# Edge terms of a graph attention stage made one stage earlier, and added by the gathers that fetch keys and values

## The reference

```python
h = relu(layernorm(x))
logit = tanh(h @ W1.T) @ w2                      # "pool" round
x = x + segment_sum(softmax_by_dst(logit[src]) * h[src], dst)
h = relu(layernorm(x))
# "multi" round: 8 heads of 16
q, k, v = h @ Wq0 + bq0, h @ Wk0 + bk0, h @ Wv0 + bv0
e = edge_attr @ We0                              # 200,000 x 16 by 16 x 128
alpha = sum(q[dst] * (k[src] + e)) / 4           # per head
h = relu(segment_sum(softmax_by_dst(alpha) * (v[src] + e), dst) + h @ Ws0 + bs0)
# "single" round: the same with one head of 128, then the sum with x
```

## Time and profile before

| | us |
|---|---|
| median of 3 runs | 8751.74 (8746.28 to 8770.22) |
| profiled execution, its own time | 8750.25 |
| its span, first to last instruction | 8748.3 |
| PE busy | 6293.5 (72%) |
| DVE busy | 5246.4 (60%) |
| POOL busy | 4508.2 (52%) |
| ACT busy | 2808.0 (32%) |
| mean granted TensorE clock | 0.816 |

### The profile page before, as it was taken

The page is one execution under the profiler, slowest core; times in us unless marked ns, Lnnn a source line. Parts: engine busy times, 40 slices in busy tenths (PEclk is TensorE's granted clock), DMA queues, the critical chain, the costliest instruction groups (busy, mean ns, idle before and its releaser), DMA issues. The chain is left out here.

```text
span 8748.3 us, 177087 instructions
## 1 busy us (share of the span) xinstructions
PE 6293.5 (72%) x37309; PEld 4520.2 (52%) x37309; DVE 5246.4 (60%) x16838; ACT 2808.0 (32%) x6528; POOL 4508.2 (52%) x4707
## 2 busy tenths in 40 slices
PE   3455565566643678787787888865778888899998
PEld 2445555555531455555555555542455555555555
DVE  5344444455555888899998998863333444444452
ACT  2222233333310233333333333321333334444441
POOL 0566666666620566655554444411556666666550
PEclk6677777888876788888888888876888989999995
DMA  2333333333333444433333333334344444444442
GB/s 60 76 73 73 75 74 76 79 79 80 81 87 108 114 109 107 107 103 101 98 96 92 92 94 86 88 85 115 86 90 91 95 96 100 100 104 107 105 101 59
DMA packets 1195650, 796.51 MB, mean 91 GB/s; under 512 B 629426, under 2 KB 1086096, under 8 KB 1194616
## 3 DMA queue, kind: packets, MB, share of 16 engines
q0 software_dynamic: 175168, 411.90, 19.0%
q1 hardware_dynamic: 1019448, 373.53, 18.2%
HBM read 715.50 MB, written 69.42 MB: 90 GB/s over the span
## 5 line engine op out<-in xcount | busy, mean ns | idle before, releaser
L686 POOL DMA_INDIRECT ring_multi<-kv_rows,src_cols x1564 | 1549.9, 991 | 1722.0 <-DVE kv L794 492.0
L1085 POOL DMA_INDIRECT ring_single<-h_rows,src_cols x1564 | 1477.4, 945 | 1275.1 <-DMA ring_single<-h_rows,src_cols 470.7
L1085 POOL DMA_INDIRECT ring_pool<-pool_rows,src_cols x1564 | 1478.5, 945 | 1004.1 <-issue 421.3
L1198 PE MATMUL ps_s_pool<-ident,row_pool 128*128 128x128 f32 x1952 | 398.5, 341 | 875.8 <-issue 854.0
L1159 DVE CUSTOM_DVE_ANT_0 masked_pool<-mask_pool,ps_s_pool,start_pool 128x512 f32<-128x512 bf16 x488 | 364.6, 747 | 846.1 <-issue 787.4
L922 PE MATMUL ps_e_multi<-w_edge,attrT 64*128 64x512 f32 x976 | 591.3, 688 | 258.7 <-DVE kv L794 256.1
L1198 PEld LDWEIGHTS ps_s_pool<-ident,row_pool 128*128 128x128 f32 x1952 | 277.6, 173 | 962.4 <-issue 961.7
L1245 ACT ACTIVATE row_pool<-ring_pool 128x520 f32 x488 | 309.0, 633 | 1415.4 <-POOLq L1076 1415.4
L1213 PE MATMUL ps_p_pool<-row_pool,probT_pool 128*128 128x129 f32 x3904 | 714.5, 342 | 61.9 <-DVE probT_pool L1172 60.1
L905 PE MATMUL ps_p_multi<-message_multi,onehot 128*128 128x136 f32 x3904 | 729.7, 347 | 0.8 <-issue 0.8
L1213 PEld LDWEIGHTS ps_p_pool<-row_pool,probT_pool 128*128 128x128 f32 x3904 | 654.9, 253 | 104.0 <-issue 103.6
(11 more groups left out here) (219 smaller groups left out, 12509.3 us busy)
## 6 DMA issues: line engine op xcount, KB each, us to landing
dst_pool<-in_dst_rows SPq DMA_DIRECT2D x488, 128.0 KB
dst_single<-in_dst_rows SPq DMA_DIRECT2D x488, 128.0 KB
query_multi<-query_parts SPq DMA_DIRECT2D x488, 96.0 KB
cols<-query_cols SPq DMA_DIRECT2D x488, 64.0 KB
ring_pool<-pool_rows,src_cols POOLq DMA_INDIRECT x1564
ring_multi<-kv_rows,src_cols POOLq DMA_INDIRECT x1564
ring_single<-h_rows,src_cols POOLq DMA_INDIRECT x1564
edge_tail<-in_edge_cols SPq DMA_DIRECT2D x488, 34.0 KB
```

The costliest lines, as they stand in the source:

```text
L686: pool.indirect_dma_start(out=ring[:, u, j, :], out_offset=None, in_=rows, in_offset=bass.IndirectOffsetOnAxis(ap=g.src_cols[:, c:c + 1], ...
L1085: pool.indirect_dma_start(out=ring[:, u, j, :], out_offset=None, in_=rows, in_offset=bass.IndirectOffsetOnAxis(ap=g.src_cols[:, c:c + 1], ...
L1198: i = T_.transpose(ps_s[p1][:, j * P:(j + 1) * P], row[:, u1, j, D + 1:D + 2].to_broadcast([P, P]), g.ident[:])
```

## The change

In the pool stage, each of the first 391 items also makes one block's edge term: SP loads 16 x 512 attributes, PE multiplies them by `We0` into one of two PSUM tiles, ACT copies to `edge_out`, and SP stores the 256 KB to `edge_rows` in HBM. In the multi stage SP lays each block's edge term twice (for key and value) into its ring slot, 512 KB written from 256 KB read, and POOL's gathers are told to add (`compute_op=ALU.add`). Gone from the multi stage are DVE's `kv` add, PE's two edge products, ACT's copy of them, and the `attr` loads. The ring has 8 slots, filled again once the block's last item has been weighted (`message`), which SP waits for in POOL's place. The `reset` and `query` loads go from SP to ACT, 4 items ahead, and `query` has 8 buffers in place of 4. DVE's product of key and query moves up to where `kv` was. The functions `edge_stage` (now `multi_stage`) and `edge_signals` also lose branches for stages that did not use them.

```diff
-QB = 4
+QB = 8
+EB = 4
+AHEAD = 4
@@ multi stage
         @block.gpsimd
-                if n >= R:
-                    pool.wait_ge(ring_read.sem, items_done + ring_read.base)
-                    settle(g, pool)
+                pool.wait_ge(prefilled[u], attrs_base[u] + (n // R + 1) * 16)
                 for j in range(J):
                     pool.indirect_dma_start(
-                        out=ring[:, u, j, :], out_offset=None, in_=rows,
+                        out=ring[:, u, j].rearrange("p a c -> p (a c)"), out_offset=None, in_=rows,
                         in_offset=bass.IndirectOffsetOnAxis(ap=g.src_cols[:, c:c + 1], axis=0),
+                        compute_op=ALU.add,
                     ).then_inc(gathered[n % 2][j], 16)
-                    if j == J - 1 and R <= n + 1 < BLOCKS:
-                        items_done = pool.value_load(...)
         @block.sync
+            for n in range(BLOCKS):
+                u = n % R
+                if n >= R:
+                    items_done = sp.value_load(g.block_ends[0:1, n - R:n - R + 1], min_val=1, max_val=ITEMS)
+                    sp.wait_ge(E["message"].sem, items_done + E["message"].base)
+                    settle(g, sp)
+                sp.dma_start(ring[:, u], g.edge_rows[n].unsqueeze(2).to_broadcast([P, J, 2, D]))\
+                  .then_inc(prefilled[u], 16)
         @block.vector
-                if multi and has(m1, ITEMS):
-                    E["edge"].wait(dve, m1)
-                    E["message"].wait(dve, m1 - 4)
+                if has(m1, ITEMS):
+                    E["query"].wait(dve, m1)
+                    E["alpha"].wait(dve, m1 - 1)
                     dve.wait_ge(blocks_ready, items.block(u, 1) + (1 + blocks_base))
-                    V.tensor_tensor(out=kv[:, u1 % 4], in0=in_ring(...), in1=ps_e[:]..., op=ALU.add)
+                    V.tensor_tensor(out=prod[:], in0=in_ring(items, u, 1, 0), in1=ps_q[:], op=ALU.mult)\
+                     .then_inc(E["prod"].sem, 1)
         @block.scalar
+            def fetch(k, u, ahead):
+                E["scan"].wait(act, k - U)
+                act.dma_start(reset[:, k % U], ...).then_inc(g.block_words_loaded[k % U], 16)
+                E["query"].wait(act, k - QB)
+                act.dma_start(query[:, k % QB]..., ...).then_inc(g.query_loaded[k % QB], 16)
@@ dense stage, only for pool
         @block.sync
+                if not single and has(n, BLOCKS):
+                    B_["edge"].wait(sp, n - U)
+                    sp.dma_start(edge_in[:, u], t["edge_cols"][0:EDGE_DIM, n * EDGES_B:(n + 1) * EDGES_B])\
+                      .then_inc(g.attrs_loaded[u], 16)
+                if not single and has(n - 6, BLOCKS):
+                    edge_store(n - 6)
         @block.tensor
+                if not single and has(n, BLOCKS):
+                    landed(pe, g.attrs_loaded, attrs_base, n, u)
+                    B_["edge_sb"].wait(pe, n - 2)
+                    for j in range(J):
+                        i = T_.matmul(ps_e[u % 2][:, j], edge_in[:, u, j * P:(j + 1) * P], w_edge[:],
+                                      start=True, stop=True)
+                    i.then_inc(B_["edge"].sem, 1)
         @block.scalar
+                k = n - 1
+                if not single and has(k, BLOCKS):
+                    B_["edge"].wait(act, k)
+                    if k >= EB:
+                        act.wait_ge(g.edge_stored[k % EB], k // EB * 16)
+                    S_.activation(edge_out[:, k % EB], ps_e[k % 2][:], ACT.Copy).then_inc(B_["edge_sb"].sem, 1)
```

More of the change, by code:

```diff
@@ L567, in tile @@
         return self._unpacked(U + u - lag, 1)
-EDGE_SIGNALS = ("rel", "onehot", "kv", "prod", "alpha", "scan", "ends", "shown", "peak", "fresh_max",
+EDGE_SIGNALS = ("rel", "onehot", "prod", "alpha", "scan", "ends", "shown", "peak", "fresh_max",
                 "drop", "kept_max", "gap", "message", "scaled", "summed",
-                "onehotT", "query", "attrT", "edge", "alphaT", "prefix", "tile_max", "edge_max",
-                "partial",
-                "onehotT_sb", "attrT_sb", "onehot32", "rows", "absent", "factor", "weight")
+                "onehotT", "query", "alphaT", "prefix", "tile_max", "edge_max",
+                "partial", "onehotT_sb", "onehot32", "absent", "factor", "weight")
+BLOCK_SIGNALS = ("edge", "edge_sb")
 def edge_signals(g):
-    g.edge = {k: Signal(sem(g, "edge_" + k)) for k in EDGE_SIGNALS}
+    g.edge = {k: Signal(sem(g, "edge_" + k)) for k in EDGE_SIGNALS + BLOCK_SIGNALS}
+    g.edge_stored = [sem(g, f"edge_stored{k}") for k in range(EB)]
     g.block_words_loaded = [sem(g, f"block_words_loaded{k}") for k in range(U)]
@@ L591, in blocks_gathered, with multi_stage @@
         g.gathered_base[k] += len(range(k, BLOCKS, 2)) * 16
[L594 removed]
+def multi_stage(g, rows, ring_blocks):
     nc, t = g.nc, g.t
     V, S_, T_ = nc.vector, nc.scalar, nc.tensor
[L600 to L603 removed]
+    E, H, R = g.edge, HEADS, ring_blocks
+    acc_w = H * HW
@@ new lines, in multi_stage @@
+        ring = sb(g, ph, "ring_multi", [P, R, J, 2, D])
+        rel = sb(g, ph, "rel_multi", [P, U, J])
+        onehot = sb(g, ph, "onehot_multi", [P, U, J, P], BF16)
+        onehotT = sb(g, ph, "onehotT_multi", [P, U, J, P], BF16)
+        reset = sb(g, ph, "reset_multi", [J * H, U, P])
+        prefix = sb(g, ph, "prefix_multi", [J * H, 2, P])
+        ends = sb(g, ph, "ends_multi", [P, 2, J, H + 1], BF16)
+        absent = sb(g, ph, "absent_multi", [P, 2, J])
+        shown = sb(g, ph, "shown_multi", [P, 2, J, H])
@@ L918, in step @@
                       .then_inc(E["prefix"].sem, 1)
-                if multi and has(n, ITEMS):
-                    E["attrT_sb"].wait(pe, n)
-                    E["kv"].wait(pe, n - 1)
-                    T_.matmul(ps_e[:], attrT[:, u % 2], w_edge[:].rearrange("k j c -> k (j c)"),
-                              start=True, stop=True).then_inc(E["edge"].sem, 1)
                 if has(m3, ITEMS):
@@ L946, in step @@
                                           start=(k == 0), stop=(k == 2))
-                        for k in range(3 if single else 0):
-                            i = T_.matmul(tail_q[:, j], onehotT[:, u, j], query[:, u % QB, k, D:ACC_W],
-                                          start=(k == 0), stop=(k == 2))
                     i.then_inc(E["query"].sem, 1)
@@ L960, in step @@
                 m3, u3, p3, f3 = n - 3, (u - 3) % U, (u - 3) % 2, (u - 3) % 4
-                if multi and has(n, ITEMS):
-                    E["attrT"].wait(act, n)
-                    E["edge"].wait(act, n - 2)
-                    S_.activation(attrT[:, u % 2], ps_s[0:J * EDGE_DIM, 0:P], ACT.Copy)\
-                      .then_inc(E["attrT_sb"].sem, 1)
                 if has(n, ITEMS):
@@ L978, in step @@
                       .then_inc(E["absent"].sem, 1)
-                if not multi and has(n, ITEMS):
-                    E["partial"].wait(act, n - U)
-                    act.wait_ge(blocks_ready, items.block(u) + (1 + blocks_base))
-                    settle(g, act)
-                    S_.activation(row[:, u, :, 0:copied], in_ring(items, u, 0, 0, copied), ACT.Copy)\
-                      .then_inc(E["rows"].sem, 1)
+                if has(n + AHEAD, ITEMS):
+                    fetch(n + AHEAD, u, AHEAD)
                 if has(m3, ITEMS):
@@ L1130, in _ @@
             rolled(sp, ITEMS, U, 0, step, items.begin, peel=ITEMS // U)
+            if not single:
+                for k in range(EB):
+                    sp.wait_ge(g.edge_stored[k], 16 * len(range(k, BLOCKS, EB)))
         @block.vector
@@ L1177, in _ @@
         def _(pe):
+            if not single:
+                pe.wait_ge(g.w_edge_loaded, 16)
             def step(n, u):
```

261 lines of the change are left out of this document (91 added, 170 removed).

## The result

The changed kernel is slower: 9631.44 us, median of 4 runs (9612.05 to 9637.2), against 8760.98 us for the kernel before in the same comparison. The ratio is 1.0991, 95% interval [1.0965, 1.1016]. The prediction was 8580 us, in a range of 8390 to 9080; the time is outside it. The profiled execution took 9634.98 us, with a span of 9633.2.

The account below looks back on a forecast made before the run. DVE was taken to bound the multi stage, with gathers next: 6.12 + 0.35 + 0.3, say 6.8 us a block, makes 2710 us, 210 less. With 40 more in the pool stage, 8750 - 170 = 8580 us, range 8390 to 9080.

Parts of the forecast that it names:

- the adding gather's price: Multi stage: adding gathers cost 0.35 us a block more on landing, with the issue kept at 0.945 us.
- The landing term: Multi stage: reading the destination too delays a gather's landing by 0 to 0.46 us, taken as 0.35.
- POOL's issues get longer: Rival, multi stage: x us more an issue adds 1564x; half as long again gives 9315 us, twice 10,060; chance 0.17.
- The prefill: Multi stage: laying edge terms into ring slots adds 0.3 us a block to landings, range 0 to 1.7.
- The pool stage: Pool stage: the added edge-term work costs 40 us more, bounded by 0 and 143 us.
- DVE: Multi stage: DVE loses 586.6 us, leaving 2030 us of work, 4.78 us an item with its idle time.
- DVE does not get faster: Rival, multi stage: DVE is held at 5.9 us an item, stage stays at 2920, time 8790 us; chance 0.09.
- Gather-bound: Multi stage: once DVE is faster, POOL and its gathers set the pace, 6.8 us a block, stage 2710 us.
- The DMA engines fill up: Rival, multi stage: 94 engine-us a block, 86% of the engines; at both upper bounds about 9270 us; chance 0.20.
- The loads on ACT: Multi stage: moving two loads to ACT, about 1.2 us an item, costs nothing.

Follow-up runs that it names:

- e1: Changed kernel with plain gathers that overwrite the prefilled edge terms, so the edge term is left out: 8709.79 us, ratio to before 0.9935.
- e6: Changed kernel with plain gathers of 64 rows instead of adding ones of 128, on another chip: multi stage 3484 us, median issue 903 ns.
- e9: Changed kernel with plain gathers and only the first 8 prefills, edge term left out: 8452.91 us, ratio to before 0.9648.
- e4: Changed kernel with only the first 8 blocks prefilled, later gathers adding onto what the slot held: 9249.69 us, ratio to before 1.0541.
- e12: Changed kernel with only the 256 KB store a block (zeros) left of the pool stage's additions: 9475.05 us, pool stage 2365 us.
- e3: Changed kernel with only the first block's edge term stored and every prefill reading it: 9449.26 us, ratio to before 1.0768.
- e7: Changed kernel with POOL waiting for its own third gather in every second block only, on another chip: multi stage 3314 us.
- e11: Changed kernel with first 8 prefills, third-gather waits every second block, and only 4 stores of zeros in the pool stage: 8896.5 us, ratio to before 1.0155.

## Why the prediction was wrong, point by point

**The step that failed first is the adding gather's price.** The sum took POOL's issue over at 0.945 us and gave the add 0.35 us on the landing. Measured: 1.549 us an issue in the median, 938 us in the stage (e1). The landing term was there too, beyond its upper end of 0.46: a landing comes 1.0 us later after its issue's end. Of that 0.31 us a block was waited for ahead of the next block, and in POOL's waits as a whole nothing, because the longer issues covered it. The rival "POOL's issues get longer" had this with its price, 1564x: x = 0.60 gives 940, and its lowest point, half as long again, stood at 9315. I gave it 0.17. Its ground was that no row showed an adding gather, which bounds the issue's cost as little as the landing's; yet I put both ends on the landing (0 to 0.46) and none on the issue, and so left 940 us out of the sum. With that x the rival gives 8580 + 940 = 9520 us; the pool stage's 221 us above the forecast, and the 86 by which the rest of the multi stage stays below it (2624 in e1 against 2710), make it 9655, near the 9631 measured. My reading of the earlier trace rows was wrong as well. Two plain gathers of 128 rows with unlike bytes show that the price isn't by the byte; they can't show that it is by the row, and e6 shows that most of it is fixed. The rule named beside that rival, in the Trainium skill's "Collectives: The Full Stack" on the bandwidth ceiling (an add sends two read descriptors for a copy's one), points the right way: between 64 and 128 rows the issue grows by 2.0 ns a row with the add and by 0.7 without. Those 1.3 ns a row are some 170 ns of the 603; the larger part, fixed, isn't in proportion to descriptors. That 9631 lies between the two times which the prediction gave for that rule is luck to this extent. On the DMA engines the trace agrees with the rule: 115 ns of engine time a row against 56.

**The prefill** was taken at 0.3 us a block in a range of 0 to 1.7; it is 0.61 under plain gathers (e1 against e9) and 0.96 under adding ones (e4), that is 375 us. The mechanism (landings come later beside other traffic) and the range were right, the size was not. A smaller misreading stands beside it: of the 1.44 us a block that I took from the earlier trace rows as the wait for the third gather the row shows 1.28, and the rest is a third issue that was longer.

**The pool stage** was taken at 40 us in a range of 0 to 143; it is 261. The term that failed is the traffic. I bounded it by the single stage's landing waits, 470.7 against 328.1, but after the change the pool stage waits 590.0, 262 more than before, as much as the stage grew. For the store alone the bound held: e12, with the engines at 0.44, waits 446.7 us and costs 122. What it left out is that the loads, products and copies come on top (e3: 385.1 us of waits, 65 us), and that together they cost more than the sum. PE's 592 us of products, which I counted as hidden, are nearly so: everything but the store costs 65 us alone, and some 74 more with it.

**DVE** came out as worked out: 2067.5 us of work (2030 forecast), and 2386 us for the stage once the gathers are out of the way, 4.89 us an item against the 4.78 of the prediction. "DVE does not get faster" is false. **"Gather-bound"** was right as a mechanism. Without its 0.35 for the add the forecast for the stage is 391 x 6.45 + 51 = 2573 us, and e1 without the add takes 2624; what it lacks is the prefill's size.

**The DMA engines fill up**: the load came as this rival summed it, but not its effect. A block takes 0.67 x 16 x 3553.6/391 = 97 engine-us where the rival had 94, and the add's second reads are 29 to 30 of them, its upper end. Their share is only 0.67 because the block, with its longer issues, takes 9.03 us; at the forecast 6.8 us it would be some 90%, by estimate. POOL's waits for landings went from 444.4/391 = 1.1 to 1.8 us a block. What an adding gather would cost whose issue were as short as the plain one, no run shows. **The loads on ACT** cost nothing that shows: in e9 DVE waits 126 us for blocks and little else.

The sum by measured terms: 1564 x 0.60 = 938 for the adding issue, -296 for all else in the multi stage (e1), 261 for the pool stage, 903 in all; measured 870 by the medians and 885 by the spans.

## What to carry to other kernels

An operation moved from an engine onto a DMA still has an engine behind it. Price the issue of the new form as well as its transfer; where no row shows that form, let the unknown issue run from its present duration to its double in the sum itself, not only in a rival, and above all where that queue is the next bound. And a wait that stays the same does not show that the transfer is as cheap: look at the queue's engine time too, which doubled here. A stage that waits for gathers to land paid here for what other queues moved at the same time, to SBUF and to HBM alike, with the engines at a share of 0.44. Before work is handed from one bound to the next, ask what the second one's margin is: early in the stage it was 0.3 us a block (1.07 items of 5.98 us against 6.12), and the changed kernel's block takes 2.9 us more.

## What the runs showed that was not expected

- An indirect gather that adds takes POOL 1549 ns to issue for 128 rows against 946 plain, at 1 KB and at 512 B a row alike; at 64 rows it is 1421 against 903. By the line through these two sizes both are mostly a fixed price for the instruction.
- The same gathers take 59 engine-us of the DMA engines a block when they add and 29 when they don't. This is nearly hidden behind the longer issues.
- A 256 KB transfer a block delays gathers as much within SBUF (2360 us) as to HBM (2365), at a mean DMA share of 0.44.
- Waiting for the third gather in every block costs 250 us with the prefill beside it (e7) and some 98 without (e4 to e11). In the dense stages the wait was already in every second block only.
- PE's busy time in the multi stage fell only from 2318 to 1948 us though it lost 591 us of products: the granted clock was 0.67 in the longer stage, against 0.83, and 0.80 in e9. PE wasn't the bound, so it cost nothing here.
